# A four-layer attention kernel: the first layer's norm residuals enter their sums as an accumulating transpose

## The reference

```python
residual = input
sa = _mha(input, input, input, sa_wq, ..., sa_wo, sa_bo, trg_mask, causal=True)
x = _layer_norm(sa + residual, ln1_g, ln1_b)
residual = x
ca = _mha(x, encoder_output, encoder_output, ca_wq, ..., ca_wo, ca_bo, src_mask, causal=False)
x = _layer_norm(ca + residual, ln2_g, ln2_b)
residual = x
h = jax.nn.relu(x @ ffn_w1 + ffn_b1)
x = _layer_norm(h @ ffn_w2 + ffn_b2 + residual, ln3_g, ln3_b)
```

## Time and profile before

| | |
|---|---|
| runs | 2757.31, 2754.66, 2752.17 us |
| profiled execution | 2753.06 us, of which its span is 2751.3 us |
| TensorE matmul, busy | 2333.3 us (85%) in 11161 records |
| VectorE, ScalarE, GpSimd, busy | 55%, 43%, 12% of the span |
| TensorE's mean granted clock | 0.895 of full speed |

### The profile page before, as it was taken

The page is one execution under the profiler, slowest core; times in us unless marked ns, Lnnn a source line. Parts: engine busy times, 40 slices in busy tenths (PEclk is TensorE's granted clock), DMA queues, the critical chain, the costliest instruction groups (busy, mean ns, idle before and its releaser), DMA issues.

```text
span 2751.3 us, 37417 instructions
## 1 busy us (share of the span) xinstructions
PE 2333.3 (85%) x11161; PEld 1616.3 (59%) x11161; DVE 1504.4 (55%) x3998; ACT 1170.6 (43%) x4001; POOL 340.6 (12%) x349
## 2 busy tenths in 40 slices
PE   6887988898888988798889988898879888875898
PEld 3555655566565665565555656565556656443596
DVE  4554666465745666566656575566656575233212
ACT  3452635264544635263536454463527353210221
POOL 0002011101111011201201011201120120112000
PEclk9998999999999999999999999999999999566555
DMA  5000000000000000000000000000000000000001
GB/s 151 1 1 13 1 1 1 12 3 1 1 1 14 1 1 1 14 1 1 1 6 10 1 1 1 14 1 1 1 6 1 1 1 1 0 0 1 0 0 30
DMA packets 24580, 20.48 MB, mean 7 GB/s; under 512 B 1699, under 2 KB 22183, under 8 KB 24359
## 3 DMA queue, kind: packets, MB, share of 16 engines
q1 hardware_dynamic: 24358, 17.78, 2.2%
HBM read 15.68 MB, written 2.10 MB: 6 GB/s over the span
## 4 chain that ended last, share of the span: by engine, by line
issue 69%; PE 13%; POOL 11%; DVE 4%; ACT 2%; SPq 0%; POOLq 0%; DMA 0%; DVEq 0%
POOL kx L564 4%; POOL rstd L541 3%; PE ps L940 2%; PE ps L647 2%; PE ps L936 2%; POOL s_probsT L569 2%; POOL main_residual L554 1%; PE ps L788 1%; PE ps L655 1%; ACT probs L978 1%; PE ps L690 1%; ACT s_probs L978 1%; PE ps L781 1%; PE ps L953 1%; POOL pool_scratch L535 1%
## 5 line engine op out<-in xcount | busy, mean ns | idle before, releaser
L978 ACT ACTIVATE probs<-ps,neg_max 128x128 f32<-128x128 f32 x1024 | 362.7, 367 | 421.2 <-DVE neg_max L1139 414.5
L978 ACT ACTIVATE s_probs<-ps,s_max 128x128 f32<-128x128 f32 x768 | 219.5, 368 | 270.2 <-DVE s_max L1139 270.1
L690 PE MATMUL ps<-keys,queries 128*128 128x256 f32 x1024 | 283.0, 400 | 29.3 <-ACT queries L972 29.3
L713 PE MATMUL ps<-probsT,values 128*128 128x256 f32 x1024 | 274.6, 391 | 3.7 <-ACT headsT L1012 2.7
L788 PE MATMUL ps<-kx,qT 32*128 32x512 f32 (+1 forms) x384 | 239.6, 706 | 34.2 <-POOL kx L564 34.2
L1139 DVE TENSOR_REDUCE neg_max<-ps 128x4 f32<-128x512 f32 x256 | 176.7, 690 | 162.2 <-PE ps L693 160.9
L1139 DVE TENSOR_REDUCE s_max<-ps 128x4 f32<-128x512 f32 x192 | 132.7, 691 | 231.9 <-PE ps L788 229.7
L690 PEld LDWEIGHTS ps<-keys,queries 128*128 128x128 f32 x1024 | 188.1, 196 | 121.2 <-issue 51.3
L541 POOL TENSOR_TENSOR rstd<-var_eps,minus_half 128x4 f32<-128x4 f32 x88 | 90.4, 1027 | 1234.9 <-DVE var_eps L1152 1234.1
L1146 DVE BATCH_NORM_STATS2 stats<-ps 128x6 f32<-128x128 f32 x352 | 78.3, 285 | 298.6 <-PE ps L655 295.0
L713 PEld LDWEIGHTS ps<-probsT,values 128*128 128x128 f32 x1024 | 176.7, 192 | 63.5 <-issue 16.7
(11 more groups left out here) (211 smaller groups left out, 4109.7 us busy)
## 6 DMA issues: line engine op xcount, KB each, us to landing
x_in<-in_x SPq DMA_DIRECT2D x8, 256.0 KB, 2.9
c_in<-in_ctx SPq DMA_DIRECT2D x8, 256.0 KB, 3.2
skip_in<-in_mask_BxS_ik SPq DMA_DIRECT2D x8, 256.0 KB, 3.2
out<-x_all SPq DMA_DIRECT2D x8, 256.0 KB, 2.3
valid_in<-in_mask_BxS_bf SPq DMA_DIRECT2D x8, 64.0 KB, 3.7
w_qkv_sa<-in_L_xattn_sa_wq SPq DMA_DIRECT2D x1, 512.0 KB
w_qkv_sa<-in_L_xattn_sa_wk SPq DMA_DIRECT2D x1, 512.0 KB
w_qkv_sa<-in_L_xattn_sa_wv SPq DMA_DIRECT2D x1, 512.0 KB
```

The costliest lines, as they stand in the source:

```text
L690: mm(bank(MAIN, item)[:, n * 256:n * 256 + 256], queries[:, c % 2, at], keys[:, c % 2, :, at], start=(n == 0), stop=False, skip_group_chec ...
L713: last = mm(bank(MAIN, item)[:, n * 256:n * 256 + 256], values[:, c // 4, b0 + n, (c % 4) * 128:(c % 4) * 128 + 128], probsT[:, u % 2, n * ...
L978: last = A(dst[:, u % dst.shape[1], h * 128:h * 128 + 128], bank(st, (tag, "s", u))[:, h * 128:h * 128 + 128], ACT.Exp, bias=src_max[:, u ...
```

## The change

`sums` takes the residual as an argument of its own. With one, the last product no longer closes the accumulation, and a matmul with the transpose flag follows it: the same l (`main_residual`), the same r (identity), the same place in PSUM, `start=False` and `stop=True`. `main` passes `main_residual` so for ln1, ln2 and ln3. Side's sums are as they were.

```diff
-            def sums(st, tag, terms):
+            def sums(st, tag, terms, residual=None):
 
                 for b in range(G):
                     dst = bank(st, (tag, "y"))[:, b * 128:b * 128 + 128]
                     todo = list(terms(b))
                     for n, (l, r) in enumerate(todo):
-                        last = mm(dst, l, r, start=(n == 0), stop=(n == len(todo) - 1))
+                        last = mm(dst, l, r, start=(n == 0), stop=(residual is None and n == len(todo) - 1))
+                    if residual is not None:
+                        last = mm(dst, token(residual, b), ident[:, :], start=False, stop=True, is_transpose=True)
                 last.then_inc(filled[st], 1)
...
                             if tag == "ln3":
                                 before_filling(i, item, *[("ffn", c) for c in range(FC0)])
-                                sums(MAIN, tag, lambda b: [(token(hidden[:, c, :], b), w_f2[:, c, :]) for c in range(FC0)]
-                                     + [(token(main_residual, b), ident[:, :])])
+                                sums(MAIN, tag, lambda b: [(token(hidden[:, c, :], b), w_f2[:, c, :]) for c in range(FC0)],
+                                     main_residual)
                             else:
                                 t = "sa" if tag == "ln1" else "ca"
                                 before_filling(i, item, *[(t, "o", u) for u in range(UNITS)])
-                                sums(MAIN, tag, lambda b: [(token(headsT[:, c, :], b), w_o[t][:, c, :]) for c in range(C0)]
-                                     + [(token(main_residual, b), ident[:, :])])
+                                sums(MAIN, tag, lambda b: [(token(headsT[:, c, :], b), w_o[t][:, c, :]) for c in range(C0)],
+                                     main_residual)
```

## The result

| | before | changed |
|---|---|---|
| first comparison, median of 5 runs each | 2754.66 us (2748.47 to 2757.31) | 2737.64 us (2731.55 to 2743.83) |
| ratio, 95% interval | | 0.9939 (0.9917 to 0.9961) |
| profiled execution, its span | 2753.06, 2751.3 us | 2743.83, 2742.1 us |
| mean granted clock of the profiled execution | 0.895 | 0.890 |
| records of TensorE's matmuls | 11161 | 11065 |

The changed kernel is faster, as forecast, and the interval of the ratio holds the forecast ratio, 2743.7/2754.66 = 0.9960. So there are two things to explain: what the change does, and why a right sum gave a wrong time.

A forecast was written before the change was run, and what follows sets the result against it. TensorE was taken to set the time at main's 24 sums. Replacing 96 matmuls of 0.223 us by turns of 0.110 gives 10.9, with one at a lower clock 11.0: 2754.66 − 11.0 = 2743.7 us, range 2739.0 to 2748.5.

The forecast's parts named there:

- What bounds the kernel: At main's 24 sums TensorE alone sets the time; VectorE's waits ending with a residual's matmul total 169.1 us.
- The price of a turn in an open sum: In main's sums, a transpose costs 0.110 us for the matmul's 0.223, without surcharge for switches; 96 save 10.9 us.
- The drain rival: TensorE drains at each switch between matmul and transpose in an open accumulation: +16.8 us, 2771.5 us; chance 5%.
- The rival of a quarter price: A turn in the sums costs a quarter of the matmul, 0.056 us, saving 16.0 us: 2738.6 us; chance 3%.
- the first two of no change: In the sums, the flag shortens nothing (2754.7 us), or turns run at half-clock price, 0.23 us (2755 us); no change together 11%.
- the third: No change because TensorE's clock gives the gain back, taking 7 us or more; the no-change cases together 11%.
- The reach of the gain: Each main sum ends 0.46 us sooner and all of it reaches the end: passes 1.37 us shorter, 11.0 us in all.
- The forecast's time: Whole kernel: median of the runs less 11.0, 2754.66 − 11.0 = 2743.7 us; chance 81%.
- The range: Whole kernel: ±4 us for one clock step in each of 8 groups, widened for the runs' spread to 2739.0 to 2748.5.
- I expect no mean shift: Shorter passes meet the clock's drops at other places, with no mean change of time, only ±4 us.

The follow-up runs named there:

- the 22 later runs: The changed kernel repeated without edit, 12 runs (2738.11 us) and later 10 runs (2738.42 us); ratio 0.9959 to the kernel before both times.
- e3: The changed kernel with the 96 transposes left out, so the sums lack the residual; ratio 0.9952 to the kernel before.
- e4: The kernel before, matmul residual kept, with one discarded turn more ahead of each accumulation; ratio 1.0015 to the kernel before.
- e1: The changed kernel once more, no edit; 2738.11 us, median of 12 runs, ratio 0.9959 to the kernel before.
- the dummies: Discarded matmuls filling some of TensorE's waits: added to the kernel before 2715.72 us (0.9879), added to the changed kernel 2689.02 us (0.9784).
- e9: The changed kernel with three discarded matmuls only at the end of a pass, behind ln3's turn; 2727.59 us, ratio 0.9911 to the kernel before.

## Why the prediction was right or wrong

- **What bounds the kernel.** Right. TensorE alone sets the time in the 24 sums: VectorE's waits for them came down by the 11.0 us, 0.46 each.
- **The price of a turn in an open sum.** Right: 0.11 us with both switches, from the nearest rows on closed sums. The drain rival (+16.8 us) would have shown as gaps around the turn, and there are none. The rival of a quarter price and the first two of no change fell with the same rows; the third, that the clock gives all of it back, fell with the 22 later runs.
- **The reach of the gain.** Right in the total: 11.0 us less waiting, ratio 0.9959 in 22 runs for a forecast of 0.9960. But the agreement is closer than the mechanism gives cause for. The passes of the profiled execution shrank by 1.1 us on average, with single ones by 0 and by 1.8, where the prediction has 1.37; with two of the four other amounts of work (e3, e4) the total is 8 and 5 us off the sum. That it is met here to 0.3 us is partly luck.
- **The forecast's time.** This is the step that failed: the forecast "is the median of the runs less 11.0". The median of three runs, 2754.66, was taken as the kernel's level. Over 63 runs that level is 2749.9, with single runs from 2740 to 2760. 2749.9 − 11.0 = 2738.9 would have met the measured 2737.6 and 2738.1 to about a microsecond. The changed kernel's level is the same in the first comparison as later, so it was the three runs of before that lay high, not the changed kernel that was faster at first. A warning was in the table: the profiled execution was 1.6 us below that median, and I dismissed it as "within the runs' own spread".
- **The range.** "±4 us" for the clock came from the passes of one trace, all of which meet the drops at nearly the same places; they say nothing of a run that starts elsewhere. One kernel's runs differ by 17 us (2730.2 to 2747.1 in e1), so medians of five still move by some microseconds. The range should have been that wide on both sides.
- **"I expect no mean shift."** True of the changed kernel, 0.3 us off, but not a rule: with e3's and e4's amounts of work the shift was 8 and 5 us, and beside the dummies 16.

The rule of the Trainium skill ("TensorE: Matmul & The Clock Gate", Part 4) that the full clock does not engage for transposes is not borne out by the changed kernel's rows either: at ln2 (1398.9 to 1406.6 us) the granted clock is 1.00, and each turn between plain matmuls takes 0.11 us, not the 0.23 of the earlier trace rows.

## What to carry to other kernels

A 128x128 float32 transpose by the identity can close an open accumulation. It costs half of the identity matmul that it replaces, with no gap at either switch; what it brings is decided by who waits for the end of the sum. When runs of one kernel differ and their mean granted clock goes with the time, three runs do not fix a level: forecast the ratio from the trace, and give the level the runs' whole scatter. And look at what TensorE does ahead of each drop of its clock: here filling 1 to 2 us of its waits with discarded matmuls brought more than four times what the change itself did.

## What the runs showed of the hardware that I had not expected

- The length of a wait does not by itself decide whether the clock drops behind it: the same 2.34 us wait was followed by 0.50 in one pass and 1.00 in the next.
- The work of a pass does not fix its length: with 1.18 us more in each pass of e4 the last passes stayed at 300.3 us, and e9's took 297.0 and then 300.4 us in one execution with the same work.
- The scatter of single runs of one kernel, 2740 to 2760 us, goes with the mean granted clock of each (0.892 to 0.901), at 1.9 us for 0.001.
